# An attention kernel on one core: queries finished in two halves, the first context chunk split in halves, and x reloads issued from ScalarE's DMA queue

## The chip, the core and the metric

The kernel runs on one core of one Trainium2 chip. The metric is the device time of one launch in microseconds (us), taken as the median of several runs; lower is better. A core has five engines with an instruction queue each: TensorE (PE, matrix multiply; PEld is its weight load, which lies beside the multiplies), VectorE (DVE), ScalarE (ACT), GpSimd (POOL) and SyncE (SP), which in this kernel only issues DMAs. Engines meet through semaphores: an instruction waits until a counter has reached a number. An engine works its own queue in order, so whatever stands behind a waiting instruction waits too.

## The reference

Two layers over 8 batches of `x` (512 channels by 1024 positions) and a context `ctx` (also 512 by 1024):

```python
q = einsum('bcn,dc->bnd', x, Wq) + bq            # d = 64
k = einsum('bcn,dc->bdn', ctx, Wk) + bk[:, None]
v = einsum('bcn,dc->bdn', ctx, Wv) + bv[:, None] # 512 rows
attn = softmax(einsum('bnd,bdm->bnm', q, k), axis=2)
x = einsum('bcm,bnm->bcn', v, attn) + x          # layer 0
# layer 1: x is the output of layer 0, x_2 is ctx
g, phi, theta = g_w @ x_2 + g_b, phi_w @ x_2 + phi_b, theta_w @ x + theta_b   # 256 rows each
W = einsum('bnc,bcm->bnm', theta.T, phi) / 1024
y = einsum('bnm,bmc->bnc', W, g.T).transpose(0, 2, 1)
out = bn_gamma * (w_w @ y + w_b - bn_mean) * rsqrt(bn_var + 1e-5) + bn_beta + x
```

## The kernel before

Everything is fp32. Each operand of a matmul is split into a high part (rounded to the matmul's format by a ScalarE copy) and a low part (what is left, subtracted on VectorE or GpSimd), and a product is the sum of three matmuls: high by high, high by low, low by high. So nearly every tile goes PSUM or DMA, ScalarE copy, VectorE or GpSimd subtract, TensorE.

The batches run one after another, 640 matmuls each. In the words of the order tables: `k` and `q` are the projections of the context and of x (128 rows come out, 64 from the weights' high part and 64 from their low part, which a ScalarE copy and VectorE additions then sum and lay down twice); `v:m` the eight blocks of values; `S:t` the eight blocks of scores (128 queries by 1024 keys); `L`, `G`, `GT`, `Y`, `M`, `B` the small products of layer 1, worked out from the Gram matrix of the context; `PV:h,c` the attention output for half h of the queries and channel chunk c (24 matmuls each, in two parts); `th` and `wy` layer 1's two last products. Batch 0 has `kv:0` to `kv:3` in place of the first, where k and four blocks of v are accumulated chunk by chunk as the context arrives.

A block of scores takes this way: VectorE finds the row maximum (`S`, L904), ScalarE takes the exponential (`S`, L755), VectorE normalizes (`n`, L908 and L910) and transposes inside 32 by 32 squares (`tr`, L919). There is one buffer `P`, so the exponential of block t waits for the transpose of block t-1. For each pair p of blocks SyncE then issues 16 DMAs (`move(b, p)`, L398), which put the squares where they belong; `move(b, 2)` waits for `tr:5` and `move(b, 3)` for `tr:7`. ScalarE and VectorE split what has landed (`T:t`, L793 and L949), and `PV:1,0` on TensorE waits for `T:7`, `PV:0,0` for `T:3`.

`x` is loaded a second time, as the residual: `load_xr` (L378 to L384) loads eight pieces of 256 KB per batch into four buffers `xr`. The first four wait for `S:7` (the buffers lie over those of the split queries), and the others for GpSimd to be through with the piece before in the same buffer. All DMAs are issued by SyncE, in one order: three moves, four pieces of x, the fourth move, three pieces, the next batch's loads, the last piece.

The order on the other engines is written out in the tables `FIRST` (batch 0) and `LATER` (batches 1 to 7), one string for each engine; a word with a plus sign belongs to the next batch. `wait(eng, name, b, i)` waits for the i-th event of that name in batch b, and `PER` says how many such events a batch has.

The query path is `do_q` on ScalarE (L723: one copy of 64 by 1024, after `q:1`), `do_q` on VectorE (L884: two additions of 64 by 1024, L887), `do_q2` on ScalarE (L737, the high part) and `do_q2` on VectorE (L894, the low part). `do_S` on TensorE (L593) waits for all of `klo` and `qlo` at block 0. The first context chunk comes in two DMAs; its high part is made in two halves (`x2a`, L695, and `x2:0`, L700) and its low part in one (`x2:0` on VectorE, L861).

Of the kernel before, what the change touches and what calls it, by code (L numbers as in the profile page):

```python
# [1095 lines left out]
```

## Time and profile before

| | us |
|---|---|
| three runs | 1046.83, 1044.41, 1046.98 |
| median | 1046.83 |
| the profiled execution, its own time | 1045.17 |
| its span in the profile | 1043.3 |
| TensorE busy | 1033.1 (99%) |
| VectorE busy | 649.5 (62%) |
| ScalarE busy | 489.6 (47%) |
| GpSimd busy | 274.3 (26%) |

The profile shows one execution. A group of instructions has a busy time, a count and a mean; the idle time before an instruction is put down to whoever released it. The ends of matmuls are modelled, and consecutive matmuls overlap: the full rate shows in the starts (two matmuls of 512 columns start 0.45 us after the two before). TensorE's granted clock is 1.00 in all stretches. "SPq" is SyncE's queue while it issues a DMA; the transfer itself comes after.

### The profile page before, as it was taken

The page shows a single profiled execution, that of the slowest core. Times are in us where ns is not written, and L with a number is a line of the kernel's source. Part 1 is how long each engine was busy: PE and PEld are TensorE (multiplying, and loading weights), DVE is VectorE, ACT ScalarE, POOL GpSimd, SP SyncE. Part 2 cuts the span into 40 slices and gives each one's busy share as a digit, 9 for nine tenths or more (in the row PEclk, how much of TensorE's full clock was granted, in tenths as well). Part 3 has the DMA queues.
Part 4 walks back from the last instruction along what each step waited for, and adds up shares of the span by engine and source line. Part 5 has one row for each costly group of instructions (what it writes and reads, how often), then busy time and mean ns, then how long its engine had stood idle before and what let it go on. Part 6 is the DMA issues. An engine that isn't in the chain of part 4 may idle for free.

```text
span 1043.3 us, 13895 instructions
## 1 busy us (share of the span) xinstructions
PE 1033.1 (99%) x5113; PEld 854.8 (82%) x5113; DVE 649.5 (62%) x922; ACT 489.6 (47%) x843; POOL 274.3 (26%) x235
## 2 busy tenths in 40 slices
PE   8999999999999999999999999999999999999998
PEld 6777888888888887888888888788887888878887
DVE  6994367844688345873558736586365863658624
ACT  7652464435554364532744327453275532655321
POOL 1311351122601226012350124501244012430220
PEclk9999999999999999999999999999999999999999
DMA  6536161361424514245242442334433344323412
GB/s 253 164 76 185 69 205 44 79 217 51 177 53 107 185 61 162 60 108 176 74 149 66 112 167 91 132 74 111 159 108 115 81 113 150 123 100 82 121 41 81
DMA packets 80771, 122.06 MB, mean 117 GB/s; under 512 B 13120, under 2 KB 46400, under 8 KB 80704
## 3 DMA queue, kind: packets, MB, share of 16 engines
q1 hardware_dynamic: 80704, 121.17, 37.8%
q8 instruction: 41, 0.67, 0.3%
q14 instruction: 26, 0.21, 0.1%
HBM read 70.79 MB, written 16.78 MB: 84 GB/s over the span
## 4 chain that ended last, share of the span: by engine, by line
PE 93%; SPq 3%; DVE 2%; POOL 1%; DMA 1%; ACT 1%; issue 1%; DVEq 0%
PE pG L653 31%; PE pG L548 15%; PE pG L664 8%; PE pG L556 6%; PE pG L674 4%; PE pT L674 4%; PE pG L589 4%; PE pG L563 4%; PE pT L495 3%; PE pS L601 2%; SPq L398 2%; PE pS L484 2%; PE pT L601 2%; PE pM L632 2%; PE pM L641 2%; POOL x2Ts L1024 1%
## 5 line engine op out<-in xcount | busy, mean ns | idle before, releaser
L653 PE MATMUL pG<-pt,vT 128*128 128x512 f32 x1536 | 354.2, 390 | 2.4 <-DVE pt L949 2.4
L653 PEld LDWEIGHTS pG<-pt,vT 128*128 128x128 f32 x1536 | 286.9, 188 | 61.3 <-issue 2.9
L1036 POOL TENSOR_TENSOR xms<-xr,xms 128x512 fp32r<-128x512 f32 x64 | 89.1, 1394 | 327.2 <-ACT xms L822 327.2
L548 PE MATMUL pG<-wv,x2s 128*128 128x512 f32 x720 | 168.6, 392 | 0.0
L548 PEld LDWEIGHTS pG<-wv,x2s 128*128 128x128 f32 x720 | 134.1, 188 | 30.2 <-issue 2.5
L978 DVE SCALAR_TENSOR_TENSOR xr<-pG,cl,xr 128x512 f32<-128x512 f32 x64 | 47.9, 748 | 170.0 <-PE pG L653 167.7
L822 ACT ACTIVATE xms<-xr 128x512 fp32r<-128x512 f32 x64 | 40.2, 629 | 180.5 <-DVE xr L978 180.5
L949 DVE TENSOR_TENSOR pt<-mv,pt 128x512 fp32r<-128x512 f32 x128 | 91.9, 769 | 39.8 <-ACT pt L793 39.6
L1032 POOL TENSOR_TENSOR ys<-yf,ys 128x256 fp32r<-128x256 f32 x32 | 28.9, 905 | 295.9 <-ACT ys L784 295.9
L793 ACT ACTIVATE pt<-mv 128x512 fp32r<-128x512 f32 x128 | 71.8, 620 | 37.5 <-PE pM L641 27.9
L664 PE MATMUL pG<-xms,wth 128*128 128x512 f32 x384 | 88.3, 389 | 0.0
L664 PEld LDWEIGHTS pG<-xms,wth 128*128 128x128 f32 x384 | 72.1, 188 | 14.9
L1024 POOL TENSOR_TENSOR x2Ts<-x2T_f,x2Ts 128x512 fp32r<-128x512 f32 x64 | 81.5, 1310 | 10.8 <-ACT x2Ts L762 10.8
L1017 POOL TENSOR_TENSOR x1s<-st,x1s 128x512 fp32r<-128x512 f32 x56 | 71.0, 1303 | 45.8 <-ACT x1s L714 45.8
L919 DVE STREAM_TRANSPOSE tp<-P 128x1024 f32<-128x1024 f32 x64 | 79.4, 1241 | 1.1
L749 ACT ACTIVATE vT<-pG 128x512 fp32r<-128x512 f32 x62 | 37.0, 598 | 78.8 <-PE pG L548 78.8
L556 PE MATMUL pG<-x2Ts 128*128 128x512 f32 x256 | 63.0, 398 | 0.2 <-POOL x2Ts L1024 0.2
L556 PEld LDWEIGHTS pG<-x2Ts 128*128 128x128 f32 x256 | 46.9, 188 | 15.5 <-issue 5.8
L762 ACT ACTIVATE x2Ts<-x2T_f 128x512 fp32r<-128x512 f32 x64 | 36.5, 623 | 44.3 <-DMA x2T_f<-in_ctx2T_dram 44.3
L755 ACT ACTIVATE P<-pT,nmax 128x1024 f32<-128x1024 f32 x32 | 35.5, 1109 | 37.2 <-DVE tp L919 36.6
L589 PEld LDWEIGHTS pG<-wpg,gram 128*128 128x128 f32 x384 | 47.4, 191 | 3.8 <-issue 3.2
L910 DVE TENSOR_SCALAR P<-P,rec 128x1024 f32<-128x1024 f32 x64 | 48.8, 762 | 2.3
(132 smaller groups left out, 1433.1 us busy)
## 6 DMA issues: line engine op xcount, KB each, us to landing
mv<-tp SPq DMA_DIRECT2D x512, 64.0 KB, 2.0
x2T_f<-in_ctx2T_dram SPq DMA_DIRECT2D x32, 512.0 KB, 4.9
xr<-in_x_dram SPq DMA_DIRECT2D x64, 256.0 KB, 3.3
st<-in_ctx_dram SPq DMA_DIRECT2D x31, 512.0 KB, 5.9
st<-in_x_dram SPq DMA_DIRECT2D x29, 512.0 KB, 4.2
out_dram<-oh SPq DMA_DIRECT2D x32, 256.0 KB, 2.0
out_dram<-xr SPq DMA_DIRECT2D x32, 256.0 KB, 7.3
x_raw<-in_x_dram SPq DMA_DIRECT2D x3, 512.0 KB, 7.7
```

Source lines behind the costliest of these rows:

```text
L548: last = mm(bank, x2s[:, l, c, 128 * m:128 * m + 128], wv[:, r, c, :], start=(c == 0 and n == 0), stop=(c == 3 and n == 2))
L556: last = mm(bank, x2Ts[:, HI, m, 128 * r:128 * r + 128], x2Ts[:, LO, m, :], start=(m == 0), stop=(m == 7))
L589: last = mm(bank[:, 0:256], gram[:, l, d, 128 * c:128 * c + 128], wpg[:, r, d, 256:512], start=(d == 0 and n == 0), stop=(d == 3 and n == 2))
L653: last = mm(bank, vT[:, l, m, 128 * c:128 * c + 128], pt(h)[:, r, m, :], start=(m == 0 and n == 0), stop=(m == 7 and n == 2))
L664: last = mm(bank, wth[:, l, c, 128 * k:128 * k + 128], xms(h)[:, c, r, :], start=(c == 0 and n == 0), stop=(c == 3 and n == 2))
L674: last = mm(bank, bm[:, l, k, 128 * c:128 * c + 128], th[:, r, k, 512 * h:512 * h + 512], start=(k == 0 and n == 0), stop=(k == 1 and n == 2))
L793: last = act(pt_half(t, HI)[k], moved(t)[k], ACT.Copy)
L919: done(eng.transpose(tp[t // 2 % 2][:, t % 2, :], P[:, :]), "tr")
L949: last = tt(pt_half(t, LO)[k], moved(t)[k], pt_half(t, HI)[k].bitcast(F), ALU.subtract)
L1017: done(tt(x1s(b)[:, LO, c, cols], st1(b, c)[:, cols], x1s(b)[:, HI, c, cols].bitcast(F), ALU.subtract), "x1lo")
L1024: done(tt(x2Ts[:, LO, m, :], x2T_raw(b, m), x2Ts[:, HI, m, :].bitcast(F), ALU.subtract), "x2Tlo")
L1036: done(tt(xms(h)[:, c, LO, :], xr[c][:, :], xms(h)[:, c, HI, :].bitcast(F), ALU.subtract), "xlo")
```

## The change

- **Queries in halves.** The copy, the additions, the high part and the low part of q each come as two instructions of 512 columns, one per half. The first copy waits for `q:0` alone, `S:0` for the first half of `qlo`, `S:1` for the second.
- **First context chunk.** VectorE makes its low part in two halves (`x2b`, then `x2:0`). `kv:0` on TensorE uses the first half at once and multiplies the second half of k's low part last.
- **Loads of x.** The eight pieces per batch are issued by ScalarE (`xr:u`), at places of its own table, with the same waits.
- **The tables.** All strings for TensorE, ScalarE, VectorE and GpSimd are written in another order.

```diff
-    t1k=1, t1q=1, khi=1, qhi=1, vhi=8, exp=8, Thi=8, Ghi=4, Lhi=4, GThi=2, Yhi=4, shi=1, s_rowc=1, s_colc=1, mthi=1, Bhi=2,
+    t1k=1, t1q=2, khi=1, qhi=2, vhi=8, exp=8, Thi=8, Ghi=4, Lhi=4, GThi=2, Yhi=4, shi=1, s_rowc=1, s_colc=1, mthi=1, Bhi=2,
...
-    kf=4, qf=2, klo=1, qlo=1, gf=36, mx=8, rec=8, norm=8, tr=8, Tlo=8, Glo=4, GTlo=2, slo=1, gsum=2, mtf=2, mtlo=1, Blo=2,
+    kf=4, qf=4, klo=1, qlo=2, gf=36, mx=8, rec=8, norm=8, tr=8, Tlo=8, Glo=4, GTlo=2, slo=1, gsum=2, mtf=2, mtlo=1, Blo=2,
...
     act=(
-        "PV:0,0 PV:0,1 T:4 T:5 T:6 T:7 PV:0,2 PV:0,3 PV:1,0 B:0 PV:1,1 B:1 PV:1,2 +x2:0 +x2:1 xc:0 th:0,0 xc:1 "
...
+        "xr:0 Y:3 S:6 S:7 mts xr:3 xr:2 T:4 T:5 PV:0,0 B:0 PV:0,1 T:6 xr:4 B:1 T:7 PV:0,2 PV:0,3 xr:6 xr:5 PV:1,0 "
...
@@ -374,14 +376,6 @@
-
-            def load_xr(b, u):
-                if u < 4:
-                    wait(eng, "S", b, 7)
-                else:
-                    wait(eng, "xlo", b, u - 4)
-                h, c = divmod(u, 4)
-                eng.dma_start(xr[c][:, :], x[b, 128 * c:128 * c + 128, 512 * h:512 * h + 512]).then_inc(s_xr[c], 16)
 
             def move(b, p):
 
...
@@ -424,17 +418,12 @@
             for b in range(NB):
                 for p in range(3):
                     move(b, p)
-                for u in range(4):
-                    load_xr(b, u)
                 move(b, 3)
-                for u in range(4, 7):
-                    load_xr(b, u)
                 if b + 1 < NB:
                     wait(eng, "Tlo", b, 7)
                     for c in range(4):
                         load_x2(b + 1, c)
                     load_x1(b + 1, 0)
-                load_xr(b, 7)
                 if b + 1 < NB:
                     for c in range(1, 4):
...
@@ -525,13 +514,20 @@
                     if c == 0:
                         wait(eng, "x2hi", 0, 0)
                         k_mm(HI, (1,))
-                    wait(eng, "x2lo", 0, c)
-                    k_mm(LO)
+                    if c == 0:
+                        eng.wait_ge(s_x2b, 1)
+                        k_mm(LO, (0,))
+                    else:
+                        wait(eng, "x2lo", 0, c)
+                        k_mm(LO)
                     for m in range(4):
                         v_mm(m, 2)
                     eng.wait_ge(s_wlo, W_V + 1 + c)
                     for m in range(4):
                         v_mm(m, 1)
+                    if c == 0:
+                        wait(eng, "x2lo", 0, 0)
+                        k_mm(LO, (1,))
                 else:
                     wait(eng, "x2lo", 0, c)
...
@@ -593,7 +589,9 @@
             def do_S(b, t):
                 if t == 0:
                     wait(eng, "klo", b)
-                    wait(eng, "qlo", b)
+                    wait(eng, "qlo", b, 0)
+                elif t == 1:
+                    wait(eng, "qlo", b, 1)
                 elif t >= 2:
                     wait(eng, "exp", b, t - 2)
...
@@ -686,6 +684,14 @@
         def _(eng):
             act = eng.activation
 
+            def do_xr(b, u):
+                if u < 4:
+                    wait(eng, "S", b, 7)
+                else:
+                    wait(eng, "xlo", b, u - 4)
+                h, c = divmod(u, 4)
+                eng.dma_start(xr[c][:, :], x[b, 128 * c:128 * c + 128, 512 * h:512 * h + 512]).then_inc(s_xr[c], 16)
+
...
@@ -720,12 +726,12 @@
                         eng.wait_ge(s_so[c], 16 * b)
                 done(act(k1[0:64, :], pS[64:128, :, :], ACT.Copy), "t1k")
 
-            def do_q(b):
-                wait(eng, "q", b, 1)
+            def do_q(b, h):
+                wait(eng, "q", b, h)
                 if b:
                     for c in (2, 3):
                         eng.wait_ge(s_so[c], 16 * b)
-                done(act(q1[0:64, :], pT[64:128, :, :], ACT.Copy), "t1q")
+                done(act(q1[0:64, 512 * h:512 * h + 512], pT[64:128, h, :], ACT.Copy), "t1q")
 
             def do_k2(b):
...
 
             def do_L(b, r):
                 wait(eng, "klo", b)
-                wait(eng, "qlo", b)
+                wait(eng, "qlo", b, 1)
                 wait(eng, "g", b, use_l(b, r))
                 done(act(gram[:, LO, r, :], bank_of(use_l(b, r)), ACT.Copy), "Lhi")
...
@@ -854,10 +860,17 @@
+            def do_x2b(b):
+                eng.wait_ge(s_x2a, 1)
+                tt(x2s[:, LO, 0, 0:512], st2(0)[:, 0:512], x2s[:, HI, 0, 0:512].bitcast(F),
+                   ALU.subtract).then_inc(s_x2b, 1)
+
             def do_x2(b, c):
+                wait(eng, "x2hi", b, c)
                 if b == 0 and c == 0:
-                    eng.wait_ge(s_x2a, 1)
-                wait(eng, "x2hi", b, c)
+                    done(tt(x2s[:, LO, 0, 512:1024], st2(0)[:, 512:1024], x2s[:, HI, 0, 512:1024].bitcast(F),
+                            ALU.subtract), "x2lo")
+                    return
                 done(tt(x2s[:, LO, c, :], st2(c)[:, :], x2s[:, HI, c, :].bitcast(F), ALU.subtract), "x2lo")
...
-            def do_q(b):
-                wait(eng, "t1q", b)
-                for h in (1, 0):
-                    done(stt(out=pT[64 * h:64 * h + 64, :, :], in0=pT[0:64, :, :], scalar=cl[0:64, 26:27],
-                             in1=q1[0:64, :], op0=ALU.add, op1=ALU.add), "qf")
+            def do_q(b, h):
+                wait(eng, "t1q", b, h)
+                for r in (1, 0):
+                    done(stt(out=pT[64 * r:64 * r + 64, h, :], in0=pT[0:64, h, :], scalar=cl[0:64, 26:27],
+                             in1=q1[0:64, 512 * h:512 * h + 512], op0=ALU.add, op1=ALU.add), "qf")
 
... 
-            def do_q2(b):
-                wait(eng, "qhi", b)
-                done(tt(qlo[:, :], pT[:, :, :], qhi[:, :].bitcast(F), ALU.subtract), "qlo")
+            def do_q2(b, h):
+                wait(eng, "qhi", b, h)
+                done(tt(qlo[:, 512 * h:512 * h + 512], pT[:, h, :], qhi[:, 512 * h:512 * h + 512].bitcast(F),
+                        ALU.subtract), "qlo")
 
             def do_v(b, m):
```

SyncE, from the third move of batch 0 on, before (`mv` is the target of the moves, `tp` the transposed blocks, `xr` the pieces of x, `st` the next batch's inputs):

```order
L398 DMA mv_124<-tp_116 32x2x256 x16
L384 DMA xr_103<-in_x_dram 128x512
L384 DMA xr_104<-in_x_dram 128x512
L384 DMA xr_105<-in_x_dram 128x512
L384 DMA xr_106<-in_x_dram 128x512
L398 DMA mv_110<-tp_119 32x2x256 x16
L384 DMA xr_103<-in_x_dram 128x512
```

and now, from the same move on:

```order
L392 DMA mv_124<-tp_116 32x2x256 x16
L392 DMA mv_110<-tp_119 32x2x256 x16
L357 DMA st_117<-in_ctx_dram 128x1024
L357 DMA st_118<-in_ctx_dram 128x1024
L357 DMA st_120<-in_ctx_dram 128x1024
```

The fourth move now follows the third with nothing between them. ScalarE in batch 0 from the exponential of block 5 on, now (`pt_86` is written by `T:0` to `T:3`, `pt_80` by `T:4` and later, `ys` by `Y`, `mts` is an operand of `B`):

```order
L761 ACTIVATE P,rsum<-pT,nmax 128x1024
L790 ACTIVATE ys<-yf 128x256
L697 ACTIVATE wo<-wo_f 128x1024
L799 ACTIVATE pt_86<-mv_124 128x8x64 x2
L693 DMA xr_104<-in_x_dram 128x512
L790 ACTIVATE ys<-yf 128x256 x2
L693 DMA xr_103<-in_x_dram 128x512
L790 ACTIVATE ys<-yf 128x256
L761 ACTIVATE P,rsum<-pS,nmax 128x1024
L761 ACTIVATE P,rsum<-pT,nmax 128x1024
L813 ACTIVATE mts<-mtf 128x512
```

The two first pieces of x are issued between the splits `T:3` and the parts `Y`; of these, the first waits for `S:7`. VectorE in batch 0 from the last x chunk to the first row maximum, before:

```order
L871 TENSOR_TENSOR x1s_first<-x_raw_115,x1s_first 128x1024
L900 TENSOR_TENSOR vT<-pG,vT 128x512 x2
L881 SCALAR_TENSOR_TENSOR kf<-pS,cl,k_99 64x256 x4
L900 TENSOR_TENSOR vT<-pM,vT 128x512
L887 SCALAR_TENSOR_TENSOR pT<-pT,cl,q_101 64x1024 x2
L892 TENSOR_TENSOR klo<-kf,khi 128x512
L896 TENSOR_TENSOR qlo<-pT,qhi 128x1024
L900 TENSOR_TENSOR vT<-pM,vT 128x512
L900 TENSOR_TENSOR vT<-pG,vT 128x512
L904 TENSOR_REDUCE nmax<-pS 128x1
```

and now:

```order
L884 TENSOR_TENSOR x1s_first<-x_raw_115,x1s_first 128x1024
L894 SCALAR_TENSOR_TENSOR kf<-pS,cl,k_99 64x256 x4
L914 TENSOR_TENSOR vT<-pG,vT 128x512
L900 SCALAR_TENSOR_TENSOR pT<-pT,cl,q_101 64x512 x2
L914 TENSOR_TENSOR vT<-pG,vT 128x512
L900 SCALAR_TENSOR_TENSOR pT<-pT,cl,q_101 64x512 x2
L905 TENSOR_TENSOR klo<-kf,khi 128x512
L909 TENSOR_TENSOR qlo<-pT,qhi 128x512
L914 TENSOR_TENSOR vT<-pM,vT 128x512 x2
L909 TENSOR_TENSOR qlo<-pT,qhi 128x512
L914 TENSOR_TENSOR vT<-pG,vT 128x512
L918 TENSOR_REDUCE nmax<-pS 128x1
```

The same work stands there in smaller pieces, `klo` and the first half of `qlo` before two of the four blocks of v. In batch 0 `tr:7` also moves: VectorE has `PV:0,0` and `mts` behind it before and ahead of it now. In batches 1 to 7 `tr:5` stood behind `n:5` and ahead of `Y:1`, and now stands behind `S:6`, `Y:1`, `T:3`, `Y:2` and `Y:3`; on TensorE `GT:0` and `GT:1` stood ahead of `S:4`, and `GT:1` now stands behind `S:5`.

## Rows read from the trace of the kernel before

**Rows 1.** Stretches of one batch: sum, busy by engine (count), granted clock, DMA.
```profile
0.00:142.30 142.30, 135.42 (x648) 109.53 (x649) 98.68 (x134) 80.09 (x131) 36.76 (x39) 1.00 0.48 153
527.00:655.24 128.24, 128.24 (x640) 106.50 (x639) 79.25 (x113) 60.12 (x104) 35.33 (x29) 1.00 0.38 115
```

**Rows 2.** Timeline of TensorE, batch 0: start, length, what, idle before.
```profile
8.52 0.73 PE L505 MATMUL pS<-x2s,wk 128*128 128x512 f32 x2 [0.83 <-DVE x2s L861]
...
23.77 2.55 PE L495 MATMUL pT<-x1s_first,wq 128*128 128x512 f32 x10 [0.40 <-DVE x1s_first L871]
...
32.79 0.49 PE L601 MATMUL pS<-khi,qhi 64*128 64x512 f32 x2 [1.04 <-DVE qlo L896]
...
53.01 0.25 PE L624 MATMUL pM<-ident,gram_f 2*128 2x2 f32 x2 [0.26 <-ACT gram_f L799]
53.62 0.52 PE L578 MATMUL pM<-ident,gram_f 128*128 128x128 f32 x3 [0.35 <-ACT gsc L803]
...
69.08 5.69 PE L653 MATMUL pG<-pt,vT 128*128 128x512 f32 x24 [0.57 <-DVE pt L949]
...
98.51 22.04 PE L653 MATMUL pG<-pt,vT 128*128 128x512 f32 x96 [1.80 <-DVE pt L949]
```

**Rows 3.** Timeline of ScalarE, batch 0.
```profile
4.41 0.63 ACT L695 ACTIVATE x2s<-st 128x512 fp32r<-128x512 f32 x1 [0.86 <-DMA st<-in_ctx_dram]
...
19.27 1.03 ACT L721 ACTIVATE k<-pS 64x1024 f32<-64x1024 f32 x1 [0.92 <-PE pS L505]
```

**Rows 4.** Timeline of VectorE, batch 0, up to the first row maximum.
```profile
22.49 1.22 DVE L871 TENSOR_TENSOR x1s_first<-x_raw,x1s_first 128x1024 fp32r<-128x1024 f32 x1
...
27.41 2.61 DVE L887 SCALAR_TENSOR_TENSOR pT<-pT,cl,q 64x1024 f32<-64x1024 f32 x2
29.94 1.57 DVE L892 TENSOR_TENSOR klo<-kf,khi 128x512 fp32r<-128x512 f32 x1
...
33.79 1.22 DVE L904 TENSOR_REDUCE nmax<-pS 128x1 f32<-128x1024 f32 x1
```

**Rows 5.** Timeline of VectorE, batch 0, T:3, tr:5, tr:7.
```profile
67.09 1.84 DVE L949 TENSOR_TENSOR pt<-mv,pt 128x512 fp32r<-128x512 f32 x2 [1.27 <-ACT pt L793]
68.86 1.23 DVE L919 STREAM_TRANSPOSE tp<-P 128x1024 f32<-128x1024 f32 x1
...
79.76 1.25 DVE L919 STREAM_TRANSPOSE tp<-P 128x1024 f32<-128x1024 f32 x1
```

**Rows 6.** Timeline of SyncE's queue, batch 0, moves 2 and 3.
```profile
70.11 10.46 SPq L398 DMA_DIRECT2D mv<-tp  x16
80.62 2.31 SPq L384 DMA_DIRECT2D xr<-in_x_dram  x4
83.04 10.33 SPq L398 DMA_DIRECT2D mv<-tp  x16
```

**Rows 7.** Chain that ended last, after the last issue of move 3.
```profile
92.78 2.00 DMA mv<-tp
...
96.60 1.77 DVE pt L949
```

**Rows 8.** Timeline of SyncE's queue, batch 4.
```profile
553.19 37.90 SPq L398 DMA_DIRECT2D mv<-tp  x48
591.12 2.22 SPq L384 DMA_DIRECT2D xr<-in_x_dram  x4
595.08 10.18 SPq L398 DMA_DIRECT2D mv<-tp  x16
```

**Rows 9.** Timeline of VectorE, batch 4: tr:5, T:7.
```profile
579.64 1.25 DVE L919 STREAM_TRANSPOSE tp<-P 128x1024 f32<-128x1024 f32 x1
...
609.33 1.45 DVE L949 TENSOR_TENSOR pt<-mv,pt 128x512 fp32r<-128x512 f32 x2 [1.74 <-ACT pt L793]
```

**Rows 10.** Chain in batch 4: PV from part PV:0,2,0 on (144 matmuls).
```profile
600.84 32.64 PE pG L653 x144
```

**Rows 11.** Issues of one line: least, median and greatest ns.
```profile
L384 SPq DMA_DIRECT2D xr<-in_x_dram x64: 327/430/1342, 80.6 to 999.3; - x64
```

More of the change, by code:

```diff
@@ L69 @@
     act=(
[5 rows of a table removed]
[6 rows of a table added]
     ),
     dve=(
[6 rows of a table removed]
[6 rows of a table added]
     ),
     pool=(
-        "x2T:0 x2T:1 x2T:2 x2T:3 x2T:4 x2T:5 x2T:6 x2T:7 s Y:0 Y:1 Y:2 Y:3 PV:0,0 PV:0,1 PV:0,2 PV:0,3 PV:1,0 "
+        "x2T:0 x2T:1 x2T:2 x2T:3 s x2T:4 x2T:5 x2T:6 x2T:7 Y:0 Y:1 Y:2 Y:3 PV:0,0 PV:0,1 PV:0,2 PV:0,3 PV:1,0 "
         "PV:1,1 PV:1,2 PV:1,3"
@@ L97 @@
     act=(
[4 rows of a table removed]
[5 rows of a table added]
     ),
     dve=(
[5 rows of a table removed]
[5 rows of a table added]
     ),
     pool=(
-        "x1:0,0 x1:0,1 x1:1,0 x1:1,1 x1:2,0 x1:2,1 x1:3,0 x1:3,1 s x2T:0 x2T:1 x2T:2 x2T:3 x2T:4 x2T:5 x2T:6 "
+        "x1:0,0 x1:0,1 x1:1,0 x1:1,1 x1:2,0 x1:2,1 x1:3,0 x1:3,1 x2T:0 x2T:1 x2T:2 x2T:3 s x2T:4 x2T:5 x2T:6 "
         "x2T:7 Y:0 Y:1 Y:2 Y:3 PV:0,0 PV:0,1 PV:0,2 PV:0,3 PV:1,0 PV:1,1 PV:1,2 PV:1,3"
@@ L235, in xattn_kernel @@
         s_nbg = sem("s_nbg")
-        s_x2h, s_x2a = sem("s_x2h"), sem("s_x2a")
+        s_x2h, s_x2a, s_x2b = sem("s_x2h"), sem("s_x2a"), sem("s_x2b")
         s_warm = sem("s_warm")
@@ L735, in do_k2 @@
                 done(act(khi[:, :], kf_at(b), ACT.Copy), "khi")
-            def do_q2(b):
-                wait(eng, "qf", b, 1)
+            def do_q2(b, h):
+                wait(eng, "qf", b, 2 * h + 1)
                 if b:
@@ L741, in do_q2 @@
                         eng.wait_ge(s_st[i], 16 * b)
-                done(act(qhi[:, :], pT[:, :, :], ACT.Copy), "qhi")
+                done(act(qhi[:, 512 * h:512 * h + 512], pT[:, h, :], ACT.Copy), "qhi")
             def do_v(b, m):
@@ L796, in do_gs @@
             def do_gs(b):
-                wait(eng, "qlo", b)
+                wait(eng, "qlo", b, 1)
                 wait(eng, "s_row", b)
@@ L829, in do_th @@
                 done(act(th[:, HI, k, 512 * h:512 * h + 512], bank_of(i), ACT.Identity, bias=thb(k)), "thhi")
-            do = dict(w=do_w, x2=do_x2, x2a=do_x2a, xs=do_xs, x1=do_x1, k=do_k, q=do_q, k2=do_k2, q2=do_q2, v=do_v, S=do_S, L=do_L, G=do_G,
+            do = dict(w=do_w, xr=do_xr, x2=do_x2, x2a=do_x2a, xs=do_xs, x1=do_x1, k=do_k, q=do_q, k2=do_k2, q2=do_q2, v=do_v, S=do_S, L=do_L, G=do_G,
                       GT=do_GT, Y=do_Y, x2T=do_x2T, s=do_s, T=do_T, gs=do_gs, gt=do_gt, mts=do_mts, B=do_B, xc=do_xc, PV=do_PV,
@@ L892, in do_k2, with do_q2 @@
                 done(tt(klo[:, :], kf_at(b), khi[:, :].bitcast(F), ALU.subtract), "klo")
-            def do_q2(b):
-                wait(eng, "qhi", b)
-                done(tt(qlo[:, :], pT[:, :, :], qhi[:, :].bitcast(F), ALU.subtract), "qlo")
+            def do_q2(b, h):
+                wait(eng, "qhi", b, h)
+                done(tt(qlo[:, 512 * h:512 * h + 512], pT[:, h, :], qhi[:, 512 * h:512 * h + 512].bitcast(F),
+                        ALU.subtract), "qlo")
             def do_v(b, m):
@@ L1001, in do_out @@
                          op0=ALU.add, op1=ALU.add), "oa")
-            do = dict(w=do_w, consts=do_consts, x2=do_x2, x1=do_x1, x2T=do_x2T, k=do_k, q=do_q, k2=do_k2, q2=do_q2, v=do_v,
+            do = dict(w=do_w, consts=do_consts, x2b=do_x2b, x2=do_x2, x1=do_x1, x2T=do_x2T, k=do_k, q=do_q, k2=do_k2, q2=do_q2, v=do_v,
                       S=do_S, n=do_n, tr=do_tr, G=do_G, G2=do_G2, GT=do_GT, Y=do_Y, T=do_T, mt=do_mt, mts=do_mts, B=do_B, PV=do_PV, th=do_th,
```

50 rows, old and new, of tables (act, dve, pe) are left out of this document.

## The prediction

> **What bounds the kernel now.** I read the page's shares first (TensorE 99% busy), then cut the span at the batches. Batches 1 to 7 are solid: a batch takes 128.24 us and TensorE is busy for 128.24 of them [rows 1]. Nothing that only makes an operand ready earlier can gain there; the number of matmuls does not change. Batch 0 takes 142.30 us with TensorE busy for 135.42 [rows 1]. Of the 6.88 us between, 1.44 pass before the first matmul at all, and the waits, listed on TensorE's timeline, are the rest: 0.83 + 0.40 + 1.04 + 0.26 + 0.35 + 0.57 + 1.80 [rows 2] are 5.25, and one of 0.19 (for the low part of the transposed context, at 36.45) makes 5.44. A wait costs somewhat more than its row, since a matmul's modelled end lies about 0.15 us behind the point where the next could start: with seven or eight waits 1.2 us. So 5.44 + 1.2 = 6.6 us is all that better order can give, 0.6% of the time. The rest of the question is how much of it comes, and whether the solid batches stay solid.
>
> Behind the waits of batch 0 stand two chains. Up to 33.8 us it is ScalarE and VectorE on the operands: ScalarE waits 0.92 us for k and copies it for 1.03 us [rows 3] ahead of the last two chunks of x, VectorE ends the last chunk's low part at 23.7 and then works almost without a break, q for 2.61 us, klo, qlo, to the first row maximum at 33.79 [rows 4]. After that it is softmax and moves: tr:5 ends at 70.09 [rows 5], move 2 is issued from 70.11 to 80.57, four pieces of x to 82.93, and move 3 from 83.04 to 93.37 although tr:7 was over at 81.01 [rows 5, 6]. Its last issue at 92.78 lands 2.00 us later, and the low part is ready at 98.37 [rows 7]; PV:1,0 has waited 1.80 us for it [rows 2].
>
> **Start.** VectorE's first work is now the half low part (512 columns where a subtraction of 1024 takes 1.22 us [rows 4]; say 0.68) and only then the low part of k's weights, 256 columns, say 0.4, which the very first matmul waits for. The half chunk is there at 5.04 [rows 3], so TensorE starts at about 6.15 where it started at 5.44: 0.7 lost. The wait at 8.52 goes: the half low part is ready long before. It held TensorE from 7.41 to 8.52, 1.1 us [rows 2]. But ScalarE now copies the second chunk and sums the first (1.05 each) ahead of the second block of v's weights, and VectorE splits the third chunk (1.2) ahead of that block's low part, so kv:1 has two new short waits, together 0.5 to 1.2. Bounds of the term: 1.1 gained to 0.8 lost. I take nothing; whatever it is, TensorE then meets q, which waits for x.
>
> **Queries.** k's copy no longer stands ahead of the chunks of x on ScalarE. The last chunk's low part then ends about 0.9 us earlier (the 0.92 idle and the 1.03 copy go, a sum of 1.05 with its read-out comes ahead), at 22.8. TensorE's q ends at 25.5, v:4 and v:5 take 5.4 more: TensorE is at S:0 at 31.0 instead of 31.6. What S:0 waits for is earlier as well: from 22.8 VectorE needs k 1.8, one v 0.6, first half of q 1.4, one v 0.6, second half 1.4, klo 0.7 to 1.5, half qlo 0.7. That is 30.0 to 30.8, by rows of twice the length [rows 4]. So S:0 starts at 31.0 and not at 32.79 [rows 2]: 1.8. S:1 has to wait for the second half of qlo, which stands behind two blocks of v, until 32.6 or so, which the exponential of block 0 hides partly: S:2 follows at 35.2 instead of 36.88. The term: 1.7, bounds 0.6 (the halves cost VectorE more than I take, the row maximum gains only the 0.9 of x) to 2.3.
>
> **Gram and first moves.** The two waits of 0.26 and 0.35 become one: the tiny transpose gt waits for a copy behind T:0, and T:0 waits for G:3, about 0.6 us. Nothing gained, 0.3 to either side. T:3, which released PV:0,0 at 69.08, hangs on tr:3, T:0 and then 16 issues of 0.64 us. T:0 is ready 1.2 us earlier, and 1.27 us in which VectorE waited for T:3's data [rows 5] fill with other work, so T:3 is done near 66.9; Y:2, which now stands behind it, frees PV:0,0's bank at 67.0. TensorE itself would be there at 66.3. PV:0,0 starts at 67.3 instead of 69.08: the gain up to here is 1.8, not a term beside the 1.7 but what is left of it with the shorter wait. Bounds 0.5 and 2.8.
>
> **Moves.** tr:5 ends at 68.6, 1.5 earlier. Move 2 takes its 10.4 us to 79.0. tr:7 has more ahead of it now: PV:0,0 and mts, 0.75 and 0.65 long, but tr:5 was earlier; I get 78.9. Move 3 follows at 79.0 where it began at 83.04 [rows 6]: 4.0 earlier, 2.4 of it the four pieces of x and the gap, the rest the chain ahead. T:7 is then ready at 94.4. TensorE arrives at PV:1,0 after the same 27.5 us of work as before (69.08 to 96.55), at 94.8. The wait of 1.80 with its 0.15 is gone.
>
> The eight issues on ScalarE take 0.43 us each as a median of the same line on SyncE, 1.34 at most [rows 11]; it has 4 to 5 us of idle time beside them in that stretch, as it waits for PV:0,0 and for moves. I count nothing. The bound is one issue of 1.34 ahead of T:7, which 0.4 us of room would not cover: 0.9 lost.
>
> **Batches 1 to 7.** The pieces of x never held a move there: they were issued from 591.12 to 593.34, and move 3 began at 595.08 because tr:7 ended then [rows 8]. So in seven batches of eight the new queue brings nothing. The table does change the room. tr:5 ended at 580.89 [rows 9] and move 2 with it; now S:6 (1.2), Y:1, T:3 (1.3), Y:2 and Y:3, which TensorE ends at 584.3, stand ahead, so tr:5 ends near 586.0. Move 2 then runs to 596.2 and move 3 to 606.5 instead of 605.26 [rows 8]. T:7 ended at 610.78 [rows 9] and PV:1,0 is due at 600.84 + 48 x 0.2267 = 611.72 [rows 10]; the room of 0.9 shrinks to between 0.8 and 0.3. I count nothing, and keep it as the main danger.
>
> **Sum.** 1.8 up to PV:0,0 and 1.8 for the wait at PV:1,0 (its 1.95, less 0.15 for what may be left) make 3.6. Against the profiled execution's own 1045.17 that is 1041.6. The median of the runs is 1.66 higher, 1046.83, so I forecast 1043.2.
>
> **Rivals.**
> *The chain of batch 0 keeps its length.* VectorE works nearly through from 23.7 to 81.0, and the change takes nothing off it: the halves add four starts, and PV:0,0 and mts now stand ahead of tr:7. If tr:7 ends near 80 and an issue on ScalarE or on SyncE is held up by 1 us, PV:1,0 waits again. For it: the idle time that goes is 2 us in all. Against it: move 3 alone is 2.0 freer (83.04 against 81.01). The gain is then 0.5 to 2.6, say 1.6: 1045.2.
> *More goes.* The start pays its 1.1 and no wait is left: up to 6.6, 1040.2; say 5.2, 1041.6.
> *Slower: T:7 in each later batch.* In steady state move 3 ends 1.3 us later and T:5, T:6 and T:7 now follow one another closely on VectorE after B:1. Where GpSimd works at the same time such a pair took 1.84 us [rows 5], not 1.3. Three pairs at 1.84 are 1.6 more than reckoned and overrun the room by about 1.1, seven times: 7.7 lost, less 3.6, that is 1050.9. It decides from 0.5 us per batch on, where the gain of batch 0 is eaten. Against it: GpSimd has only one piece to subtract in that stretch.
> *No effect.* If neither half of q is what S:0 waits for, and tr:7 sets move 3 as before, the time stays: that is the lower end of the first rival.
>
> **How the numbers follow.** A change of under 0.3%, 3.1 us, can't be told from none here. My forecast (gain 2.6 to 4.6) gets 0.53, and 0.35 of it lies beyond 3.1; more goes 0.10, all faster; the chain that keeps its length 0.23, all within 0.3%; slower 0.14, of which 0.04 stays within 0.3%. Faster 0.45, same 0.45, slower 0.10. The forecast's own range is 1042.2 to 1044.2. With a median of three runs that differ by 2.6 us, the range that holds the time 8 times in 10 is 1040.3 to 1047.6.
>
> **What would show it.** In the changed profile: S:0 near 31.0 with hardly a wait, and a short one before S:1; PV:0,0 near 67.3; move 3 right behind move 2, at 79; no wait at PV:1,0; batch 0 of about 138.7 us; batches 1 to 7 still 128.24 each. A wait for pt at PV:1,0 in these would prove the slower rival; an issue of well over 0.64 us in a move while ScalarE issues would prove the shared generator. The forecast is wrong if batch 0 is not 3 us shorter, or if a later batch is over 128.5.

## The result, and the profile after

The changed kernel takes 1049.20 us (median of 12 runs, 1047.61 to 1051.88), the kernel before beside it 1046.44 (12 runs, 1044.41 to 1047.49). The ratio is 1.0034, with a 95% interval of 1.0026 to 1.0043: slower by 0.3%, where 1043.2 was forecast. The profiled execution took 1047.61 us, its span is 1045.7.

Stretches of one batch, cut at the first matmul of k (length; busy time of TensorE, its weight loads, VectorE, ScalarE, GpSimd, with counts; granted clock; DMA share; GB/s). [Rows 1] are cut 0.15 us later, so the first line has batch 0 of the kernel before once more, by the same cut; then batches 0, 1 and 4 of the changed kernel:
```profile
0.00:142.15 142.15, 135.27 (x648) 109.38 (x648) 98.68 (x134) 80.09 (x131) 36.61 (x39) 1.00 0.48 153
...
0.00:140.34 140.34, 135.31 (x647) 108.99 (x648) 97.03 (x138) 80.53 (x134) 37.91 (x40) 1.00 0.49 157
140.34:269.82 129.48, 128.44 (x639) 106.43 (x638) 80.33 (x116) 60.81 (x106) 33.52 (x29) 1.00 0.37 115
...
527.64:656.03 128.39, 128.39 (x640) 106.41 (x638) 79.33 (x116) 60.93 (x106) 35.52 (x30) 1.00 0.37 116
```
Batch 0 gained 1.8 us, not 3.6. And the batches that were to stay at 128.24 did not: two (1 and 2) take 129.47 on average, four (3 to 6) 128.38, and the last stretch is 1.2 longer than before. What TensorE waited for says why (us in all, times, longest):
```profile
PE pG L651 <- DVE pt L963: 4.8, 4, 1.7
PE pT L679 <- DVE warm L1020: 1.4, 1, 1.4
PE pM L622 <- ACT gram_f L805: 0.8, 1, 0.8
```
The first row is the wait at PV:1,0 for `pt`, the low part of the moved blocks (T:7), once in batch 0 (1.70) and once each in batches 1, 2 and 7 (1.04 or 1.05). Such a wait costs its row and some 0.2 more. The sum: 3 x 1.25 + 4 x 0.14 - 1.8 = 2.5 us, as the two spans differ (1045.7 against 1043.3).

TensorE in batch 0 of the changed kernel, where [rows 2] has before:
```profile
5.99 0.50 PE L494 MATMUL pS<-x2s,wk 128*128 128x512 f32 x1 [0.34 <-DVE wk L850]
...
31.09 0.50 PE L599 MATMUL pS<-khi,qhi 64*128 64x512 f32 x2
...
67.32 3.02 PE L651 MATMUL pG<-pt,vT 128*128 128x512 f32 x12
...
96.70 1.62 PE L651 MATMUL pG<-pt,vT 128*128 128x512 f32 x6 [1.70 <-DVE pt L963]
```
The first three are as forecast (6.15, 31.0, 67.3); the fourth should have stood at 94.8 without a wait. The chain that led to it, from move 3's last issue on:
```profile
89.91 3.06 DMA mv<-tp
...
92.99 1.16 ACT pt L799 x2
...
94.17 0.04 DVE pt L963
94.21 0.57 issue
94.78 1.78 DVE pt L963
```
The last transfer takes 3.06 us to land (before 2.00 [rows 7]), and of VectorE's pair of subtractions the second takes 1.78 us. That second one was as long before (1.77 [rows 7]). The pair for T:7 in batch 0, before and then changed:
```profile
95.99 2.37 DVE L949 TENSOR_TENSOR pt<-mv,pt 128x512 fp32r<-128x512 f32 x2 [1.21 <-ACT pt L793]
...
94.17 2.38 DVE L963 TENSOR_TENSOR pt<-mv,pt 128x512 fp32r<-128x512 f32 x2 [0.83 <-ACT pt L799]
```

### The profile page after: what moved, and what is told of

The parts are those of the page before. It is cut to its first block, busy times and chain, and to the rows that moved or that the text cites. A ratio compares the mean times of both kernels' runs of the same rounds, so it can differ in the third digit from the quotient of the medians.

```text
span 1045.7 us, 13950 instructions
## 1 busy us (share of the span) xinstructions
PE 1034.3 (99%) x5113; PEld 853.7 (82%) x5113; DVE 651.6 (62%) x947; ACT 494.5 (47%) x859; POOL 273.0 (26%) x235
## 4 chain that ended last, share of the span: by engine, by line
PE 92%; DVE 3%; SPq 2%; ACT 1%; DMA 1%; issue 1%; ACTq 0%
PE pG L651 29%; PE pG L544 16%; PE pG L662 8%; PE pG L552 6%; PE pG L672 4%; PE pT L672 4%; PE pG L585 4%; PE pG L559 4%; PE pT L484 3%; PE pS L599 3%; PE pS L473 2%; DVE pt L963 2%; PE pT L599 2%; PE pM L630 2%; SPq L392 2%; PE pM L639 2%
## 5 line engine op out<-in xcount | busy, mean ns | idle before, releaser
L963 DVE TENSOR_TENSOR pt<-mv,pt 128x512 fp32r<-128x512 f32 x128 | 94.3, 787 | 42.1 <-ACT pt L799 42.1
L914 DVE TENSOR_TENSOR vT<-pG,vT 128x512 fp32r<-128x512 f32 x62 | 42.6, 687 | 17.1 <-ACT vT L755 16.4
L585 PE MATMUL pG<-wpg,gram 128*128 128x256 f32 x384 | 49.6, 285 | 0.1
```

The costliest lines, as they stand in the source:

```text
L585: last = mm(bank[:, 0:256], gram[:, l, d, 128 * c:128 * c + 128], wpg[:, r, d, 256:512], start=(d == 0 and n == 0), stop=(d == 3 and n == 2))
L963: last = tt(pt_half(t, LO)[k], moved(t)[k], pt_half(t, HI)[k].bitcast(F), ALU.subtract)
```

## What an ordinary and a stretched subtraction look like

VectorE, then GpSimd and ScalarE in batch 1 of the changed kernel (140.34 + 77 to 86), from T:4 to T:7:
```profile
218.27 2.41 DVE L963 TENSOR_TENSOR pt<-mv,pt 128x512 fp32r<-128x512 f32 x2 [4.58 <-ACT pt L799]
220.60 0.74 DVE L992 SCALAR_TENSOR_TENSOR xr<-pG,cl,xr 128x512 f32<-128x512 f32 x1
221.26 4.77 DVE L963 TENSOR_TENSOR pt<-mv,pt 128x512 fp32r<-128x512 f32 x6
```
```profile
218.83 1.29 POOL L1050 TENSOR_TENSOR xms<-xr,xms 128x512 fp32r<-128x512 f32 x1 [9.91 <-ACT xms L828]
223.88 1.61 POOL L1050 TENSOR_TENSOR xms<-xr,xms 128x512 fp32r<-128x512 f32 x1 [3.75 <-ACT xms L828]
```
```profile
222.13 0.63 ACT L799 ACTIVATE pt<-mv 128x512 fp32r<-128x512 f32 x1 [1.28 <-DMA mv<-tp]
```
T:4 is two subtractions of 0.68 each; as GpSimd starts at 218.83, the second ends 1.1 later. T:5 to T:7 are six, 3.7 us, of which one takes 1.77, again beside GpSimd. The same place in batch 4 (VectorE, then GpSimd):
```profile
608.56 3.69 DVE L963 TENSOR_TENSOR pt<-mv,pt 128x512 fp32r<-128x512 f32 x6
```
```profile
610.91 2.49 POOL L1050 TENSOR_TENSOR xms<-xr,xms 128x512 fp32r<-128x512 f32 x1 [3.48 <-ACT xms L828]
```
Here the six keep their 3.69 us and GpSimd's subtraction takes 2.49 for 1.3. So one of the two always pays (a span of GpSimd is rough in the profile, but 1.3 comes back in the rows where it runs alone), and batches 1, 2 and 7 are those in which VectorE did. The Trainium skill (SBUF — State Buffer, SBUF: two separate sides) has this as an exclusive lock on the ports that VectorE and GpSimd share: whoever starts first keeps it for the instruction. The lengths agree: 0.68 becomes 1.77, or 1.3 becomes 2.49, as if one instruction had waited for the other to end. Both can be stretched too: GpSimd's took 1.61 in batch 1, above, and 1.75 in batch 7, where it came in while one of VectorE's was running and then held up the next. That the earlier start decides is not what all rows show. In batch 6 GpSimd's row starts 0.18 us before VectorE's last subtraction, and yet it is GpSimd's that is long. What decides it, no run shows (VectorE, then GpSimd):
```profile
868.34 0.68 DVE L963 TENSOR_TENSOR pt<-mv,pt 128x512 fp32r<-128x512 f32 x1
```
```profile
868.16 2.01 POOL L1050 TENSOR_TENSOR xms<-xr,xms 128x512 fp32r<-128x512 f32 x1 [3.96 <-ACT xms L828]
```

A stretched subtraction is not new in the later batches. The kernel before has one in each of them, at no cost. VectorE, then GpSimd in its batch 4, where six subtractions (T:4 to T:6) take 4.80 us:
```profile
602.13 4.80 DVE L949 TENSOR_TENSOR pt<-mv,pt 128x512 fp32r<-128x512 f32 x6 [3.21 <-ACT pt L793]
```
```profile
604.78 1.60 POOL L1036 TENSOR_TENSOR xms<-xr,xms 128x512 fp32r<-128x512 f32 x1 [6.46 <-ACT xms L822]
```
Behind them VectorE waited 1.74 us for T:7's data [rows 9], so the 1.1 us vanished in idle time. In the changed kernel T:4 starts 77.92 us into a batch instead of 75.29, is stretched in every batch, and VectorE has no idle time left between T:4 and T:7.

TensorE is due at PV:1,0 84.64 us into a batch. With 4.77 the last subtraction ends at 85.7, with 3.69 at 84.6, and the matmul starts 0.14 us behind that end. In the second case this costs only 0.12: in the rows of single matmuls the last one ahead starts at 612.05, the first of PV:1,0 at 612.39, two starts that are 0.227 apart otherwise.

## Experiments

Eleven kernels ran, five rounds each, with the kernel before at 1045.16, 1045.01 and 1044.91 us in the three groups (the ratios are to these). "LATER" and "FIRST" are the tables of batches 1 to 7 and of batch 0.

**B:1 taken back.** On TensorE B:1 had moved behind PV:0,2,0, and T:4 waits for it on ScalarE (line 797).
```diff
 LATER pe
-PV:0,1,0 B:0 PV:0,1,1 PV:0,2,0 B:1 PV:0,2,1
+PV:0,1,0 PV:0,1,1 B:0 B:1 PV:0,2,0 PV:0,2,1
```

> The changed kernel with B:0 and B:1 back together ahead of PV:0,2,0 in batches 1 to 7 (TensorE's table alone). Theory A (the low parts T:4 to T:7 start too late, because T:4 waits for B:1, and a pair is stretched from 1.3 to 2.4 us where GpSimd subtracts at the same time): B:1 ends 2.7 us sooner in a batch, T:4 to T:6 are through before T:7's data are there, PV:1,0 waits in no later batch; 1045 to 1046 us, 3 to 4 below the changed kernel. Theory B (T:7's data land too late, since two queues issue DMAs): the data come when they came, about 81.6 us into a batch, and PV:1,0 still waits 0.3 to 1 us in some batches; 1048 us or more.

Measured: 1050.28 us, ratio 1.0046 [1.0033, 1.0058]. T:4 is 2.7 us earlier, but T:7 waits for its data. VectorE and ScalarE in batch 1 (which starts at 139.84):
```profile
219.91 2.48 DVE L963 TENSOR_TENSOR pt<-mv,pt 128x512 fp32r<-128x512 f32 x4
223.16 2.40 DVE L963 TENSOR_TENSOR pt<-mv,pt 128x512 fp32r<-128x512 f32 x2 [0.77 <-ACT pt L799]
```
```profile
221.97 0.63 ACT L799 ACTIVATE pt<-mv 128x512 fp32r<-128x512 f32 x1 [4.35 <-DMA mv<-tp]
```
The data land 82.1 us into the batch, and the pair that follows is stretched, as ScalarE's PV:0,2, which starts GpSimd, stands right behind T:7. All seven later batches have a wait at PV:1,0, 0.20 to 1.06 us long. The late B:1 alone is not the cause.

**GpSimd kept off T:4.**
```diff
 LATER act
-PV:0,0 T:4 PV:0,1 T:5
+PV:0,0 PV:0,1 T:4 T:5
```

> The changed kernel with ScalarE's PV:0,1 ahead of T:4 in batches 1 to 7, so that GpSimd's subtraction of that piece is over before T:4 starts. Theory A: the pair T:4 takes 1.3 instead of 2.4 us, all that follows comes 1.1 us sooner, and the wait of 1.04 us at PV:1,0 goes in every batch: 1045 to 1046.5 us. Theory B: no change from the changed kernel, 1049 us.

Measured: 1050.71, ratio 1.0054 [1.0041, 1.0068]. T:4's pair took 1.29 us as expected, T:7's then waited 0.32 for data and took 2.40. The stretch only moved from one pair to the other, and all seven later batches wait at PV:1,0, 0.20 to 1.24 us.

**Pieces of x issued by SyncE again**, at the places of the kernel before, the tables as changed.
```diff
 LATER act, FIRST act
-xr:0 ... xr:7
 SyncE
+for u in range(4): load_xr(b, u)      # behind move 2; xr:4..6 behind move 3, xr:7 behind the context
```

> The changed kernel with the loads of x issued by SyncE again, at the places they had (four between moves 2 and 3, three after move 3, one after the next batch's first x load). Theory A: in batches 1 to 7 move 2 ends late now, so the four issues (2.3 us) push move 3 and T:7's data by 2.3 us, from 81.6 to about 84 us into a batch; PV:1,0 waits 1.5 to 3 us in all seven: 1059 to 1068 us. Theory B: SyncE's issues run without a second queue and the data land earlier by what the sharing cost; the four issues still cost 2.3, net 1 to 1.5 us later per batch, waits under 1.5 us: 1052 to 1058 us.

Measured: 1104.01, ratio 1.0561, far beyond both. SyncE's queue in batch 1:
```profile
204.82 10.17 SPq L399 DMA_DIRECT2D mv<-tp  x16
215.04 2.03 SPq L385 DMA_DIRECT2D xr<-in_x_dram  x4
219.94 10.99 SPq L399 DMA_DIRECT2D mv<-tp  x16
```
The new table has VectorE's PV:0,0 ahead of tr:7. PV:0,0 needs a piece of x that now stands behind move 2, so tr:7 waits for a move that it has nothing to do with, and move 3 starts 2.9 us after the queue is free. PV:1,0 waits 4.7 us in this batch and 28.6 in all eight batches. These waits are not the whole loss. TensorE also waits 7.5 us in the later batches for banks that VectorE's PV steps free (`xr`, longest 1.95) and 2.9 once for `mts`, and the granted clock fell to 0.984 over the span, where it is 0.999 or 1.00 in the other profiles. What is shown is that the new order needs the second queue.

**All of batches 1 to 7 in the old order**, halves side by side, x issued by ScalarE; batch 0 as changed.
```diff
 LATER pe, act, dve, pool
-(changed order)
+(order of the kernel before; q -> q:0 q:1, q2 -> q2:0 q2:1; act: mts xr:0..3, PV:0,3 xr:4..6, PV:1,0 xr:7)
```

> The changed kernel with the order of batches 1 to 7 as in the kernel before on every engine (the halves of q next to one another, the loads of x still on ScalarE). Both theories: batches of 128.24 us without a wait, batch 0 as in the changed kernel (1.8 us shorter than before): 1044.5 to 1045.5 us, 4 below the changed kernel. If the batches stay longer than 128.3 it is not the order but the halves or the second queue.

Measured: 1043.61 (11 runs), ratio 0.9987 [0.9978, 0.9996]. Every later batch is 128.24 us again. So the loss is in the order of the later batches, all of it, and neither in the halves nor in the queue.

**tr:5 taken back**, and **tr:5 with B:1**, in the changed kernel.
```diff
 LATER dve
-n:5 S:6 Y:1 T:3 Y:2 Y:3 tr:5 S:7
+n:5 tr:5 S:6 Y:1 T:3 Y:2 Y:3 S:7
```

> The changed kernel with one word of VectorE's table for batches 1 to 7 moved: tr:5 stands right behind n:5 again, ahead of S:6, Y:1, T:3, Y:2 and Y:3. It should then end about 4 us earlier in a batch, moves 2 and 3 with it, and T:7's data should land near 80 us into the batch instead of 81.4 to 82.0. Theory A (the late move is the cause of the waits): the three waits of 1.04 us at PV:1,0 go; only 7 x 0.15 us for the transposes of the Gram matrix is left over the old batches; median 1044.5 to 1046.5. Theory B (VectorE's own chain behind B:1 is the cause, one pair of T:4 at 2.4 us from 77.8 and one more pair stretched by GpSimd among T:5 to T:7, whenever the data come): T:7 still ends at 85.5 in the batches in which GpSimd comes in first, three to seven waits of 1.0 us remain; median 1048 to 1051.

> tr:5 back behind n:5 on VectorE and, on TensorE, B:0 and B:1 together ahead of PV:0,2,0 again, in batches 1 to 7 of the changed kernel. B alone (measured) brought T:4 forward by 2.7 us and left waits of 0.5 to 1.4 for data that landed at 81.4 to 82.0. Theory C (each of two causes is enough for a wait: the late move and the late B:1): with both taken back no wait is left in batches 1 to 7, even where T:7's pair takes 2.4 us, since it starts by 81.3; batches of 128.4 us, median 1044.3 to 1045.8. Theory A gives the same here but the same for tr:5 alone too. Rival (the order on ScalarE, PV:0,2 behind T:7, is enough by itself to make a wait): 0.3 to 1 us in each batch, median 1047 to 1051.

Measured: tr:5 alone 1052.41 (6 runs), ratio 1.0068 [1.0056, 1.0080]; both 1046.26, ratio 1.0008 [0.9999, 1.0017]. With tr:5 alone, ScalarE and VectorE in batch 1 (it starts at 141.83):
```profile
222.53 0.63 ACT L799 ACTIVATE pt<-mv 128x512 fp32r<-128x512 f32 x1 [0.21 <-DMA mv<-tp]
```
```profile
222.75 4.79 DVE L963 TENSOR_TENSOR pt<-mv,pt 128x512 fp32r<-128x512 f32 x6
```
T:7's data are there at 80.7 and it changes nothing: VectorE begins T:5 at 80.9 as before, GpSimd comes 1.1 us sooner and now wins in all seven batches, each with a wait of 1.05. My theory A, that taking back the late move is enough, is refuted: with the late B:1 alone the waits stay, and with the late move alone (the first of these runs) they stay too. With both taken back six waits of 0.20 are left.

**GpSimd made to wait**, the direct test of the stretch; tables as changed.
```diff
 GpSimd, do_PV
+                if b and (h, c) == (0, 2):
+                    wait(eng, "Tlo", b, 7)
```

> The changed kernel, all tables as they are; only GpSimd's subtract of PV:0,2 waits in batches 1 to 7 until VectorE has done T:7, so that the two cannot run at the same time. Theory B (the waits of 1.04 us at PV:1,0 are the 1.08 us by which GpSimd's subtract stretches one of VectorE's operations among T:5 to T:7): T:5 to T:7 take 3.7 us in every batch, every batch is 128.4 us, no listed wait at PV:1,0 outside batch 0; span about 1042.4, median 1043.8 to 1045.5. Theory A (the late move is the cause): T:7's data still land at 81.4 to 82.0 us, so nothing changes, three or more waits, median 1047.5 to 1050.

Measured: 1045.10 (11 runs), ratio 1.0000 [0.9991, 1.0008], so 0.3% faster than the changed kernel. All later batches are 128.37 to 128.46 us, and no wait at PV:1,0 is listed in them. VectorE, then GpSimd in batch 1 (it starts at 141.01):
```profile
221.93 3.69 DVE L963 TENSOR_TENSOR pt<-mv,pt 128x512 fp32r<-128x512 f32 x6
```
```profile
225.76 1.29 POOL L1052 TENSOR_TENSOR xms<-xr,xms 128x512 fp32r<-128x512 f32 x1 [4.97 <-DVE pt L963]
```
The data land as late as before the edit, T:4 is as late and still stretched, and yet the waits are gone: the 1.04 us were the stretched subtraction behind it. The span is 1043.5 and not 1042.4. Most of that is batch 0, which started late in the profiled execution (first matmul at 6.51) and ended 0.7 us later than the changed kernel's.

**The load of x alone, and the halves on top**, in the kernel before.
```diff
 FIRST act, LATER act
+xr:0 xr:1 xr:2 xr:3 behind mts; xr:4 xr:5 xr:6 behind PV:0,3; xr:7 behind PV:1,0   (SyncE's eight loads go)
```

> The kernel before with the pieces of x issued by ScalarE and nothing else: four behind mts, three behind PV:0,3, one behind PV:1,0, in all batches; the tables otherwise as they were. If it is as my sum had it (SyncE's four issues of x and the gap stood between tr:7 and move 3): in batch 0 move 3 starts at 81.0 instead of 83.04, T:7's data land at 91.5 to 93.4, the wait of 1.80 us at PV:1,0 falls to 0 to 0.4 and VectorE's wait of 2.21 for x goes; batches 1 to 7 stay at 128.24; median 1043.5 to 1045. Rival (issues on one queue hold up those on the other, or the pieces of x take the moves' bandwidth): move 3 takes 1 to 2 us longer and the gain is under 0.7; median 1045 to 1047. Second rival (loads of x waiting for their semaphore keep ScalarE from T:4 or T:7): waits in every batch, over 1047.

> The kernel before with the pieces of x issued by ScalarE (measured 1042.97) and, added to it, the halves in the old order: x2b right ahead of x2:0, q:0 and q:1 side by side, q2:0 and q2:1 side by side, in all batches. Theory E (halves help by themselves): the wait of 0.6 to 0.8 us for the first chunk's low part goes and S:0 starts up to 0.7 us earlier, since it needs the first half of qlo only; median 1042.0 to 1042.8. Rival (side by side the halves only add four starts to VectorE; S:0's wait falls but S:1's appears): within 0.4 of xr_only; 1042.6 to 1043.4. Batches 1 to 7 128.24 in both.

Measured: x alone 1042.97 (12 runs), ratio 0.9977 [0.9968, 0.9985]; with the halves 1042.34 (8 runs), 0.9971 [0.9960, 0.9981]. Batch 0 of each:
```profile
0.00:140.07 140.07, 134.61 (x647) 108.90 (x648) 96.94 (x134) 80.06 (x131) 37.03 (x39) 1.00 0.49 155
```
```profile
0.00:139.44 139.44, 134.56 (x648) 109.05 (x648) 96.68 (x138) 80.70 (x133) 36.98 (x39) 1.00 0.49 156
```
By the same cut (142.15 before) the queue is worth 2.1 us in batch 0, more than the 1.8 of the whole change there, and the halves perhaps 0.6 (the intervals overlap). With x alone ScalarE takes T:7 at 93.01 with data that landed no sooner than in the changed kernel, but VectorE's PV:0,2 stands between, and the pair takes 1.28.

**Batch 0 mended**, in the kernel with the old later batches, and then with the old start.
```diff
 FIRST act
-T:6 xr:4 B:1 T:7 PV:0,2 PV:0,3
+T:6 PV:0,2 B:1 T:7 xr:4 PV:0,3
 FIRST dve
-T:5 T:6 PV:0,2 T:7
+T:5 PV:0,2 T:6 T:7
```

> Batch 0 of the changed kernel with batches 1 to 7 in the old order (measured 1043.6), and in batch 0: on VectorE PV:0,2 ahead of T:6, on ScalarE PV:0,2 right behind T:6 and the load xr:4 behind T:7. GpSimd's subtract of PV:0,2 then runs at 91.7 to 93.0, off T:7's pair, and no piece of x is in flight while move 3 lands. Theory D (the missing 1.8 us of batch 0 is 1.08 from the stretched pair and about 1 from the last landing of 3.06 instead of 2.00 us): T:7 ready at 94.5 to 95.0, wait at PV:1,0 0 to 0.3 instead of 1.7; median 1041.7 to 1042.6. If the landing does not depend on xr:4: data at 92.97 still, ready at 95.5, wait 0.6, median 1042.5 to 1043. If neither counts: 1043.6.

> best1 (measured 1042.56, batch 0 of 139.53 us of which the start lost 0.4 + 0.66 + 0.25 us in three waits) with the old order of ScalarE and VectorE up to the chunks of x in batch 0: k's weights first, sums behind the splits, and the half low part x2b right behind the weights. If the start is worth what its waits show: first matmul at 5.4 to 5.7, no wait behind it until q, q starts at 21.2 to 21.7; median 1041.3 to 1042.2. Rival (the start is set by the landing of the context chunks and what is gained is given back at S:0, which hangs on the last chunk of x): q starts earlier but waits for x, S:0 at the same time as in best1, median 1042.3 to 1042.8.

Measured: 1042.56 (8 runs), ratio 0.9974 [0.9964, 0.9983], and 1042.44 (11 runs), 0.9974 [0.9965, 0.9983]. No wait over 0.13 us is left at PV:1,0 in batch 0, whose length is 139.53 and
```profile
0.00:139.15 139.15, 135.85 (x647) 108.75 (x648) 97.23 (x138) 80.19 (x133) 37.17 (x40) 1.00 0.50 157
```
That is of the second kernel; both edits were made together, but the rows of the first part them. From the start of move 3's last issue to the end of T:7 it takes 5.26 us, where the changed kernel took 6.65 (89.91 to 96.56 above). The landing is 1.07 of this: 1.99 us instead of 3.06. It goes with the load `xr:4`. The last transfer of batch 0's move 3 took 3.0 to 3.4 us in all seven profiles in which ScalarE issues `xr:4` 0.3 to 0.9 us before that transfer is issued, and 2.0 in all six without such a load (the kernel before among them). Only 0.3 is left for the subtractions, because the stretch moved once more, to T:6. VectorE in the first kernel, T:6 and T:7 together (four would take 2.5 us unstretched):
```profile
92.02 3.75 DVE L963 TENSOR_TENSOR pt<-mv,pt 128x512 fp32r<-128x512 f32 x4 [0.87 <-ACT pt L799]
```
The wait fell by 1.6 us and batch 0 by 0.84 (140.37 with the old later batches, 139.53 here), as q began 0.7 us later in this execution. That the old start is better by itself can't be told from these two medians. The kernel with x and the halves and the two of this section are the best, 0.26 to 0.29% faster than the kernel before, and can't be told from one another.

## Why the prediction was wrong, point by point

The forecast was 3.6 us gained; the spans of the two profiled executions say 2.5 us lost. Two terms failed: the later batches, counted at nothing, cost 4.3 us, and the 1.8 us at PV:1,0 in batch 0 did not come.

- *Start*: first matmul at 5.99 (forecast 6.15), the wait of 0.83 gone, two new ones of 0.39 and 0.24. Right, within the bounds.
- *Queries*: S:0 at 31.09, no wait, S:2 at 34.99 (31.0 and 35.2). Right, only that no wait is listed before S:1 either.
- *Gram and first moves*: one wait of 0.75 in place of two (0.6), PV:0,0 at 67.32 (67.3). Right.
- *Moves*: tr:5 and tr:7 ended within 0.5 us of the forecast and move 3 followed move 2. TensorE arrived at PV:1,0 when forecast, at 94.8. But T:7 was ready at 96.56, not 94.4. The 94.4 was the 98.37 of [rows 7] moved forward by the 4.0 that move 3 was to gain, so it held a stretched pair already, and the pair is not what failed: it took 2.37 us before and 2.38 after. What failed was that the rest of this chain would keep its length and place. Move 3's last issue started at 89.91, 1.2 us later than reckoned (move 2 began 0.3 late and took 0.5 longer, and move 3 began 0.96 late), and its landing took 3.06 instead of 2.00, with a piece of x in flight that had not been there before. That is 2.2 us, 0.4 of it covered by the room and 1.7 left as a wait.
- *Eight issues on ScalarE, counted at nothing*: they took 334 to 463 ns each, the longest well under the 1.34 feared, and none stood ahead of T:7's copy for longer than that. Their issue time was nothing, as forecast. What one of the transfers did to the landing of move 3 was not in the sum.
- *Shared generator*, the skill's rule: with x alone on ScalarE, move 3 followed tr:7 and batch 0 gained 2.1 us, where a loss of 1.3 would have left 0.8. Moves 2 and 3 took 10.41 and 10.54 us there although ScalarE issued four pieces beside them, against 10.46 and 10.33 before [rows 6]. No issue of a move that lay beside one of ScalarE's took over 0.62 us in that run. In the changed kernel one of 13 did (1.29 at 719.58), but so did 15 others over 0.7, up to 1.94, with no issue of ScalarE beside them, so it proves nothing. In batch 2 of the changed kernel the 32 issues of moves 2 and 3 took 21.59 us, where two times [rows 8]'s 10.18 are 20.4. That 1.2 us is a single issue, and the kernel before, with one queue, has one like it at the same place. So no row bears out a loss by the second queue's issues (changed, then before):
```profile
344.30 1.73 SPq L392 DMA_DIRECT2D mv<-tp  x1
...
344.35 1.80 SPq L398 DMA_DIRECT2D mv<-tp  x1
```
- *Batches 1 to 7*: this step failed and turned the sign of the sum. I counted nothing; the term measured 4.3 us, three times 1.25 and four times 0.14. tr:5 came where I put it (59.1 us into batch 1, forecast 59.0), but that was not what took the room. T:7's data came on average 0.4 us later than before. The room went on VectorE: T:4 waits for B:1, which now stands behind PV:0,2,0 on TensorE, so it starts 2.6 us later, and its pair is stretched by 1.1. Where the forecast left a room of 0.3 to 0.8 us there is 0.03 (84.61 against 84.64), and any further stretch is paid in full.
- *The rival "Slower: T:7 in each later batch"*, given 0.14, named the right place and the right kind of thing, GpSimd beside VectorE's pairs. That its 1.1 us per batch is near the 1.25 measured is luck: it came from three pairs longer by 0.54 each, less a room of 0.5, and the rows have one subtraction longer by 1.1 with no room. It expected seven such batches; this execution has three. The spans of the changed kernel's 12 runs, 1045.7 to 1050.0, would fit three to seven batches with such a wait, but only one of them has a profile, so this is not shown. What I held against it, "GpSimd has only one piece to subtract in that stretch", is exactly what did it: one piece is enough.

## What to carry to other kernels

Where VectorE and GpSimd both work on SBUF, look for an operation in the rows that takes twice or more its usual time, and ask what hides it. Here a wait of 1.74 us for data hid a stretch of 1.1 in every batch, and a new order that started the same work 2.6 us later laid it bare. The robust repair was to make the engine off the critical path wait; moving one word or two of a table only moved the stretch to another pair, in three runs. A table reordered to help one stage is best split by stage in the test: here the first batch gained and seven batches, which had nothing to gain, each risked a wait. And of a change of several parts, run the one that removes work from a busy queue by itself: it held 2.0 of the 2.6 us (medians) that the best version gains.

## What the runs showed of the hardware that was not expected

- Which of VectorE and GpSimd is stretched can change from batch to batch with the same instructions: in batches 1, 2 and 7 VectorE paid 1.1 us, in 3 to 6 only GpSimd did (1.3 became 2.0 to 2.5). With tr:5 taken back T:7's data came 0.7 to 1.7 us sooner, VectorE was stretched all seven times, and the kernel was slower for it (1052.41).
- The time of an issue did not go by the queue: the pieces of x took 334 to 689 ns (median 443) on ScalarE's queue in the kernel before's order, and 327 to 1342 (median 430) on SyncE's [rows 11]. In the changed kernel, where most are issued singly or in twos, the median was 335.
- A load of 256 KB issued on one queue 0.3 to 0.9 us before the last transfer of a move on the other went with a landing of 3.0 to 3.4 us (seven profiles); without it the landing took 2.0 (six).
- The start of batch 0 varies: with the new order of the start q began anywhere from 21.61 to 23.34 us in nine profiled executions, with the old one from 21.40 to 21.80 in four. The landing of the last chunk of x for batch 0 is part of it (18.3 to 19.6 us in the nine, three of them over 19.2 with q from 22.66 on; 18.2 to 18.7 in the four) and not all (18.4 with q at 22.67), so that the order makes the difference is not shown.
